# The last stage of an eight-stage network as one course of four token pairs, with a store for each pair and two instructions of the quantisation on GpSimd

## What is computed

```python
def _quantize_activations(x, bits=ACT_BITS):
    pos = 2 ** (bits - 1) - 1
    neg = 2 ** (bits - 1)
    scale = jnp.clip(jnp.max(jnp.abs(jax.lax.stop_gradient(x)), axis=-1, keepdims=True), 1e-05) / pos
    q = jnp.clip(jnp.round(x / scale), -neg, pos) * scale
    return x + jax.lax.stop_gradient(q - x)
...
H = jnp.asarray(_hadamard(IN_FEATURES))
xh = x @ H
xq = _quantize_activations(xh)
wq = _ternary_quantize_ste(weight)
return jnp.einsum('bsi,oi->bso', xq, wq)
...
x = x + _L3_ffn_ref(_layernorm(x, axis=-1), L3_ffn_weight)
```

## Time and profile before

| what | us |
|---|---|
| median of 3 runs | 5413.29 |
| lowest and highest of the 3 | 5395.52, 5438.34 |
| the profiled execution: its span, first to last instruction | 5413.8 |

### The profile page before, as it was taken

The page is one execution under the profiler, slowest core; times in us unless marked ns, Lnnn a source line. Parts: engine busy times, 40 slices in busy tenths (PEclk is TensorE's granted clock), DMA queues, the critical chain, the costliest instruction groups (busy, mean ns, idle before and its releaser), DMA issues. The chain is left out here.

```text
span 5413.8 us, 111310 instructions
## 1 busy us (share of the span) xinstructions
PE 4614.7 (85%) x45206; PEld 3112.5 (57%) x45501; DVE 2884.4 (53%) x9511; ACT 2082.3 (38%) x4120; POOL 576.5 (11%) x1302
## 2 busy tenths in 40 slices
PE   5489999999999965889989889899778979788784
PEld 3357777777777753555555555555444756566463
DVE  6634555555555535777766677666455224433433
ACT  2223333333333312665665666566433322212221
POOL 3300111111111112111111111111000000000000
PEclk8789999999999976999999999999889989878786
DMA  0000000000000011000000000000010010000000
GB/s 26 23 18 2 2 2 2 2 2 2 2 2 2 2 61 54 4 4 6 7 6 4 4 9 4 6 1 1 1 40 1 1 44 1 1 1 1 1 1 9
DMA packets 32272, 49.22 MB, mean 9 GB/s; under 512 B 8244, under 2 KB 23638, under 8 KB 31136
## 3 DMA queue, kind: packets, MB, share of 16 engines
q1 hardware_dynamic: 28448, 38.27, 2.2%
q10 hardware_dynamic: 2304, 2.11, 0.1%
q0 software_dynamic: 1024, 1.78, 0.1%
HBM read 37.72 MB, written 4.19 MB: 8 GB/s over the span
## 5 line engine op out<-in xcount | busy, mean ns | idle before, releaser
L2299 DVE TENSOR_REDUCE l_m<-psum 128x2 bf16<-128x512 f32 x768 | 503.8, 692 | 148.8 <-PE psum L1904 146.5
L2175 ACT ACTIVATE l_probs<-psum,l_mcol 128x1024 f32<-128x1024 f32 x384 | 406.3, 1109 | 159.2 <-PE psum L1942 159.2
L1184 PE MATMUL psum<-g_gx,ident 128*128 128x128 f32 x1536 | 416.0, 389 | 18.0
L1173 PE MATMUL psum<-g_still,ident_bf 128*128 128x256 bf16 (+3 forms) x1551 | 391.5, 281 | 1.7 <-PEq L58 1.7
L1904 PE MATMUL psum<-l_kb,l_qmb 32*128 32x256 bf16 x1536 | 295.4, 273 | 56.1 <-DVE l_m L2299 52.4
L1252 ACT ACTIVATE g_th<-g_pre 128x256 f32<-128x256 f32 x512 | 191.7, 417 | 314.3 <-DVE g_pre L1285 314.3
L1184 PEld LDWEIGHTS psum<-g_gx,ident 128*128 128x128 f32 x1536 | 279.4, 195 | 12.8
L1942 PE MATMUL psum<-l_qm,l_keys 32*128 32x256 f32 x3072 | 265.1, 418 | 13.3 <-issue 13.3
L2186 ACT COPY l_heads_out<-psum 128x256 f32<-128x256 f32 (+1 forms) x292 | 130.0, 445 | 369.8 <-PE psum L1968 186.3
L1285 DVE TENSOR_TENSOR g_pre<-g_encp,psum 128x256 f32<-128x256 f32 x512 | 192.8, 418 | 132.9 <-PE psum L1202 122.4
L2299 DVE TENSOR_REDUCE l_cm<-psum 128x4 bf16<-128x256 f32 x400 | 166.0, 427 | 179.8 <-PE psum L1904 179.6
(11 more groups left out here) (567 smaller groups left out, 9761.9 us busy)
## 6 DMA issues: line engine op xcount, KB each, us to landing
s_w<-in_S_w SPq DMA_DIRECT2D x16, 256.0 KB, 5.0
f_w<-in_F_w SPq DMA_DIRECT2D x2, 2048.0 KB, 12.5
l_wf<-in_L_W SPq DMA_DIRECT2D x6, 576.0 KB, 3.8
l_w<-in_L_W SPq DMA_DIRECT2D x1, 3072.0 KB, 10.6
l_nw<-in_L_nw SPq DMA_DIRECT2D x1, 2304.0 KB, 8.0
l_wc<-in_L_W SPq DMA_DIRECT2D x6, 384.0 KB, 3.0
h_w<-in_H_W ACTq DMA_DIRECT2D x16, 129.0 KB, 3.0
h_w<-in_H_W SPq DMA_DIRECT2D x16, 129.0 KB, 3.0
```

Of the source, the lines that this page charges most:

```text
L1173: pe.matmul(psum[:, bank, 0:cols], cst["ident_bf"][:], still[:, 0:cols], start=True, stop=True)
L1184: pe.matmul(psum[:, bank, 0:P], cst["ident"][:], repeated(gx(gate, s)), start=True, stop=False)
L2175: act.activation(probs[:, u % 2, chunk, :].rearrange("p (g n) -> p g n", g=GROUP), psum[:, 0:GROUP, S * chunk:S * chunk + S], ACT.Exp, bia ...
L2299: dve.tensor_reduce(place, psum[:, c.bank(("max", u, g)), 0:x.tiles * x.width] .rearrange("p (t k) -> p t k", t=x.tiles), AX.X, ALU.min)\
```

## The change

The stage becomes one pass without a loop. All buffers of a pair, and the PSUM banks (now two for each of the four kinds), are there twice, and pair p uses number p % 2. The instructions of the four pairs are written one behind the other on each engine, in an order that interleaves the pairs: VectorE begins with the statistics of pairs 0 and 1 and their `z`, then rounds the weights, and so on, as at the end of the diff. The waits for `p >= 2` are for the buffers' other user. The last two instructions of the quantisation, `q - xh` and the sum with `xh`, go from VectorE to GpSimd (`passed`), with a new semaphore `q_scaled` that VectorE sets behind the scaling. The store of a pair is issued by SyncE as soon as its addition is done, 256 KB each, and the pass in `program` with the one store goes. Line numbers with + are of the new kernel's text; arithmetic and types stay the same.

```diff
-n0 = norm_buffers(sb, "n0")
-z, zT, xh = sb("z", [P, PT, D]), sb("zT", [P, PTOK]), sb("xh", [P, PT, D])
+        norms = [norm_buffers(sb, f"n{i}") for i in range(2)]
+        z, zT, xh = sb("z", [P, 2, PT, D]), sb("zT", [P, 2, PTOK]), sb("xh", [P, 2, PT, D])
+        hi, lo, scale, rec = (sb(n, [P, 2, PT]) for n in ("hi", "lo", "scale", "rec"))
+        q, qT = sb("q", [P, 2, PT, D]), sb("qT", [P, 2, PTOK])
+
+        Z_BANK, H_BANK, Q_BANK, R_BANK = 0, 2, 4, 6
+
+        def tokens(p):
+return X[:, PT * p:PT * p + PT, :]
+
+        with engines_pass(nc) as (block, sig):
+@block.sync
+def _(sp):
+    sp.dma_start(hada[:], dram["c_hadamard"]).then_inc(sig["hadamard_load"], 16)
+    sp.dma_start(wt[:], dram["T3_w"]).then_inc(sig["weights_load"], 16)
+    out = dram["out"].rearrange("(t p) d -> p t d", p=P)
+    for p in range(PAIRS):
+        sp.wait_ge(sig["tokens_ready"], p + 1)
+        sp.dma_start(out[:, PT * p:PT * p + PT, :], tokens(p)).then_inc(sig["stored"], 16)
+    sp.wait_ge(sig["stored"], 16 * PAIRS)
...
+    def transformed(p):
+        pe.wait_ge(sig["normed"], p + 1)
+        if p >= 2:
+            pe.wait_ge(sig["zT_ready"], p - 1)
+        turn_tensor(pe, cst["ident"], psum[:, Z_BANK + p % 2, :], lambda t: z[:, p % 2, t, :])\
+            .then_inc(sig["z_turned"], 1)
...
+        pe.wait_ge(sig["zT_ready"], p + 1)
+        if p >= 2:
+            pe.wait_ge(sig["xh_taken"], p - 1)
+        for t in range(PT):
+            last = pe.matmul(psum[:, H_BANK + p % 2, P * t:P * t + P], zT[:, p % 2, P * t:P * t + P], hada[:],
+                             start=True, stop=True)
+        last.then_inc(sig["xh_ready"], 1)
...
+    def multiplied(p):
+        pe.wait_ge(sig["q_ready"], p + 1)
+        if p >= 2:
+            pe.wait_ge(sig["qT_ready"], p - 1)
+        turn_tensor(pe, cst["ident"], psum[:, Q_BANK + p % 2, :], lambda t: q[:, p % 2, t, :])\
+            .then_inc(sig["q_turned"], 1)
...
+    transformed(0)
+    transformed(1)
+    pe.wait_ge(sig["ternary_ready"], 1)
+    pe.transpose(psum[:, R_BANK, 0:P], wn[:], cst["ident"][:]).then_inc(sig["w_turned"], 1)
+    multiplied(0)
+    transformed(2)
+    multiplied(1)
+    transformed(3)
+    multiplied(2)
+    multiplied(3)
...
+    def passed(p):
+        pool.wait_ge(sig["q_scaled"], p + 1)
+        qs, xs = q[:, p % 2, :, :], xh[:, p % 2, :, :]
+        pool.tensor_tensor(qs, qs, xs, ALU.subtract).then_inc(sig["q_apart"], 1)
+        pool.wait_ge(sig["q_apart"], p + 1)
+        pool.tensor_tensor(qs, qs, xs, ALU.add).then_inc(sig["q_ready"], 1)
+
+    root(0)
+    root(1)
+    root(2)
+    passed(0)
+    root(3)
+    passed(1)
+    passed(2)
+    passed(3)
...
+    def transformed(p):
+        act.wait_ge(sig["z_turned"], p + 1)
+        act.copy(zT[:, p % 2, :], psum[:, Z_BANK + p % 2, :]).then_inc(sig["zT_ready"], 1)
+        act.wait_ge(sig["xh_ready"], p + 1)
+        if p >= 2:
+            act.wait_ge(sig["q_ready"], p - 1)
+        act.copy(xh[:, p % 2, :, :].rearrange("p t d -> p (t d)"), psum[:, H_BANK + p % 2, :])\
+            .then_inc(sig["xh_taken"], 1)
...
+    act.wait_ge(sig["weights_load"], 16)
+    act.activation(wabs[:], wt[:], ACT.Abs, accum_out=wscale[:]).then_inc(sig["abs_sum_ready"], 1)
+    transformed(0)
+    transformed(1)
+    act.wait_ge(sig["w_turned"], 1)
+    act.copy(wqT[:], psum[:, R_BANK, 0:P]).then_inc(sig["wqT_ready"], 1)
+    multiplied(0)
+    transformed(2)
+    multiplied(1)
+    transformed(3)
+    multiplied(2)
+    multiplied(3)
...
+            last = dve.tensor_scalar(qs[:, t, :], qs[:, t, :], POS, sc[:, t:t + 1], ALU.min, ALU.mult)
+        last.then_inc(sig["q_scaled"], 1)
+
+    def added(p):
+        dve.wait_ge(sig["product_ready"], p + 1)
+        dve.tensor_tensor(tokens(p), tokens(p), psum[:, R_BANK + p % 2, :].rearrange("p (t d) -> p t d", t=PT), ALU.add)\
+            .then_inc(sig["tokens_ready"], 1)
+
+    statistics(0)
+    statistics(1)
+    normed(0)
+    normed(1)
+    ternary_weights()
+    statistics(2)
+    quantised(0)
+    normed(2)
+    statistics(3)
+    quantised(1)
+    normed(3)
+    added(0)
+    quantised(2)
+    added(1)
+    quantised(3)
+    added(2)
+    added(3)
...
-        with nc.Fori(0, PAIRS) as pair:
-with engines_pass(nc) as (block, sig):
...
-        steps.after(last)
-        steps.after(dve.tensor_tensor(q[:], q[:], xh[:], ALU.subtract))
-        dve.tensor_tensor(q[:], q[:], xh[:], ALU.add).then_inc(sig["q_ready"], 1)
...
-        with engines_pass(nc) as (block, sig):
-@block.sync
-def _(sp):
-    sp.dma_start(dram["out"].rearrange("(t p) d -> p t d", p=P), X[:]).then_inc(sig["stored"], 16)
-    sp.wait_ge(sig["stored"], 16)
```

More of the change, by code:

```diff
@@ new lines, in _, with root @@
+            @block.gpsimd
+            def _(pool):
+                def root(p):
+                    w = norms[p % 2]
+                    pool.wait_ge(sig["var_ready"], p + 1)
+                    pool.tensor_scalar(w["veps"][:], w["mv"][:, :, 1:2], EPS, 1.0, ALU.add, ALU.mult).then_inc(sig["veps_ready"], 1)
+                    pool.wait_ge(sig["veps_ready"], p + 1)
+                    pool.tensor_tensor(w["rstd"][:], w["veps"][:], cst["mhalf"][:], ALU.pow).then_inc(sig["rstd_ready"], 1)
+                def passed(p):
[12 more added lines that the diff above has]
+                passed(3)
@@ new lines, in statistics, with normed @@
+                def statistics(p):
+                    w = norms[p % 2]
+                    for t in range(PT):
+                        last = dve.bn_stats(w["stats"][:, t, :], X[:, PT * p + t, :])
+                    steps.after(last)
+                    for t in range(PT):
+                        last = dve.bn_aggr(w["mv"][:, t, :], w["stats"][:, t, :])
+                    last.then_inc(sig["var_ready"], 1)
+                def normed(p):
+                    w = norms[p % 2]
+                    dve.wait_ge(sig["rstd_ready"], p + 1)
+                    for t in range(PT):
+                        last = dve.tensor_scalar(z[:, p % 2, t, :], X[:, PT * p + t, :], w["mv"][:, t, 0:1],
+                                                 w["rstd"][:, t, :], ALU.subtract, ALU.mult)
+                    last.then_inc(sig["normed"], 1)
@@ new lines, in quantised @@
+                def quantised(p):
+                    xs, qs = xh[:, p % 2, :, :], q[:, p % 2, :, :]
+                    top, low, sc, inv = (b[:, p % 2, :] for b in (hi, lo, scale, rec))
+                    dve.wait_ge(sig["xh_taken"], p + 1)
+                    dve.tensor_reduce(top, xs, AX.X, ALU.max)
+                    steps.after(dve.tensor_reduce(low, xs, AX.X, ALU.min))
+                    steps.after(dve.tensor_scalar(low, low, -1.0, 1e-5, ALU.mult, ALU.max))
+                    steps.after(dve.tensor_tensor(top, top, low, ALU.max))
+                    steps.after(dve.tensor_scalar(sc, top, 1.0 / POS, None, ALU.mult))
+                    steps.after(dve.reciprocal(inv, sc))
+                    if p >= 2:
+                        dve.wait_ge(sig["q_turned"], p - 1)
+                    for t in range(PT):
+                        last = dve.tensor_scalar(qs[:, t, :], xs[:, t, :], inv[:, t:t + 1], ROUND, ALU.mult, ALU.add)
```

89 lines of the change are left out of this document (27 added, 62 removed).

## The result

The changed kernel takes 5368.91 us (median of 6 runs, 5352.31 to 5380.75), the kernel before 5419.73 in the same comparison (6 runs, 5395.52 to 5438.34). The ratio is 0.9906, with a 95% interval from 0.9879 to 0.9932. The forecast was 5368.0, 0.84% faster than the three runs known then; measured are 0.94% less.

The account below looks back on a forecast made before the run. VectorE's queue, then an uncovered tail, was to bound the new stage: 5321.1 + 30.8 + 0.3 + 5.1 + 0.6 = 5357.9, tail 7.1, then 0.1 + 2.5 + 0.7 gave 5368.3 us. Forecast 5368, own range 5363 to 5373 (61%).

Parts of the forecast that it names:

- What bounds the stage: Last stage before the change: one serial chain, engines never busy together, 18.95 us of chain in each 20.1 to 20.35 us pair.
- VectorE's queue: VectorE's own work in the new stage up to the scaling of pair 3: 30.8 us.
- The meeting: z of pairs 2 and 3 waits on VectorE for GpSimd's two instructions: 2.54 us per pair, 5.1 us for two.
- The small instructions of pair 3: 128x4 quantisation instructions on VectorE meet GpSimd's addition for pair 2: 0.6 us more.
- TensorE's clock: TensorE's clock, 0.50 before, expected to rise to the upper level mid-stage and be at the lower in the tail.
- the case named for a low clock everywhere: If TensorE's clock stays low throughout, pair 3's xh comes 2.1 us late on VectorE: +1.5 us.
- The tail: From the last scaling to the last addition, GpSimd 2.6, transposes 1.15, copy 0.6, product 2.1, addition 0.7: 7.1 us.
- The store: After the last addition: 0.1 us to issue, 2.5 for the last 256 KB to land, 0.7 to span end; three stores hidden.
- No collision: Rival, 22%: GpSimd's q instructions and VectorE's z don't hold each other up; end at 5363.6 us.
- More waits: Rival, 13%: low clock throughout (+1.5), small instructions and reductions held up (3.9), last store of 5.1 (+2.6): 5376 us.
- No overlap: Rival, 2%: one of the new waits chains the pairs as before; end at 5411.5 us.
- the fetch of straight-line code: Rival, 2%: each of some 120 VectorE instructions waits for its own fetch; at 0.5 us each 5428 us.

Follow-up runs that it names:

- e7: Changed kernel with both quantisation instructions back on VectorE and one 1 MB store in its own pass; last addition 40.96 us, end 47.43 us behind SyncE's first issue.
- e5: Changed kernel with unread identity transposes filling TensorE's gaps; last addition 40.89 us, end 44.55 us behind SyncE's first issue.
- e1: Changed kernel with the two quantisation instructions back on VectorE for all four pairs; last addition 40.95 us, end 44.08 us behind SyncE's first issue.
- e6: Changed kernel with the two quantisation instructions on VectorE for pair 3 alone; last addition 42.76 us, end 45.86 us behind SyncE's first issue.
- e3: Kernel before, loop kept, only the two quantisation instructions moved to GpSimd; last addition 91.01 us, end 97.63 us behind SyncE's first issue.
- e9: Changed kernel with GpSimd's two for pairs 0 and 2 alone and VectorE and TensorE reordered; last addition 39.58 us, end 43.02 us behind SyncE's first issue.
- e8: Kernel of e9 plus identity transposes in TensorE's gaps; last addition 39.31 us, end 42.74 us behind SyncE's first issue; ratio 0.991 against the kernel before.
- e10: Kernel of e8 with 30, 12, 24, 10 fillers ahead of q; last addition 37.17 us, end 40.55 us behind SyncE's first issue; ratio 0.9894 against before.

## Why the prediction was right, and which of its terms were not

- **What bounds the stage.** Right. It was one chain with VectorE idle for over half of a trip; the course alone brings 45.4 us (e7).
- **VectorE's queue**, 30.8 us up to the last scaling. From 5316.09 to 5352.70 are 36.61 us; less 4.06 of waits in z, 2.35 for xh and 0.49 for roots, 29.7 remain. The term was 1.1 too large, since I added gaps that aren't there: an instruction that waits for nothing starts some 0.08 us before its forerunner's end in the timeline (z at 5328.83, the scaling's end at 5328.91).
- **The meeting**, 5.1 us. The mechanism was right, at the two places named; each group was prolonged by 2.03, not 2.54. The earlier trace rows held the better price: 3.98 less 1.11 is 2.87 for three GpSimd instructions, 0.96 each and 1.9 for two, and I took 1.27 each. The first z instruction and the hand-over between GpSimd's two fit into the time that I had given to the waits.
- **The small instructions of pair 3**, 0.6 us. Not there in the changed kernel: GpSimd's addition for pair 2 (the second of its two) was over by then. The effect itself exists (0.89 against 0.17 in e5).
- **TensorE's clock.** Wrong in the step "I expect the middle to rise to the upper level". It stayed at 0.50 with TensorE busy for 3 of 4 us and waiting some 0.5 to 1 us in between. Extra work in those gaps raises it (e5); what in it does so, the shorter gaps or the added work, the runs don't tell apart, since fillers change both. So the case named for a low clock everywhere came true, at a higher price: VectorE waited 2.35 us before the reductions of pair 3, where the prediction had +1.5. The clock is not the only cause of this wait. It is gone in e5, where the clock rose; but in e1, whose clock is as low, it is 0.21. There q of pair 1, which TensorE turns and multiplies ahead of z of pair 3, is done 22.3 us behind SyncE's first issue instead of 24.1, and xh of pair 3 follows at 30.4 instead of 32.2. So GpSimd's part made TensorE late as well.
- **The tail**, 7.1 us. Measured 7.33 (5352.70 to 5360.03). That this part depends on which engine has the last pair's two instructions was in the rows, but I priced it within the change and never asked for it by itself: 1.2 us (e6).
- **The store**, 3.3 us, was 3.77, because the last one landed in 2.9 instead of 2.5.
- **The sum.** 47.3 us for the stage (5368.3 less 5320.98) against 47.76. The errors were +1.1, +1.0 and +0.6 on one side and -2.35 (xh), -0.2 (roots), -0.2 (tail) and -0.5 (store) on the other, and they cancel to half a microsecond. That is luck: the forecast is better than its terms. It is luck as well that the median of whole times lies within 1 us of the forecast, with single runs of one kernel 28 and 43 us apart, and with 0.83% saved in the stage where the whole times say 0.94%.
- **The rivals.** "No collision" fell by the trace (3.14 and 3.15 us). "More waits" holds in one item, the clock. "No overlap" and the fetch of straight-line code fell: VectorE's first instruction came 0.05 us behind SyncE's first issue, and no idle stretch lacks a releaser behind it.
- What the prediction did not say, and should have: that the change without its GpSimd part would be better, by 3.0 us to the last addition and 3.7 to the end. The terms were there: 5.1 for the meeting, 1.2 in the tail, against 1.42 a pair on a queue that has waits anyway.

## What to carry to other kernels

Price each part of a compound change by itself, also when the sum is well in favour: here 45.4 and 3.35 us of gain carried 3.7 us of loss, far below the scatter of whole times. Moving work to a slower second engine costs its full price in the last link of a chain (1.23 us here) and wherever nothing runs beside it (1.2 us a pair in e3). That it pays where the first engine has other work that doesn't meet it is a guess that no run here proves: e9 is built on it, but changed the order too. When runs scatter by more than the gain, compare the edited stage by the profile, from a point that is the same in both; and price both levels before a clock is counted on to rise: here TensorE was busy for about 3 of 4 us, with waits of 0.5 to 1 us between the bursts, and stayed at 0.50.

## What the runs showed of the hardware that I had not expected

Extra work made the stage faster: fillers without any use took 3.1 us off the changed kernel, because four transposes fell from 1.11 to 0.66 us and a product from 2.07 to 1.16. How many are enough must be tried: one layout of them (e8) brought the last addition 0.27 us forward over e9, another (e10) 2.41. And the last store of 256 KB landed in 2.3 us where VectorE had produced the last q, and in 2.9 to 3.1 where GpSimd had; that is not explained.
